# Cell and shared experts of a gated cross-attention stack in one block, chunk 0 ahead of the last pairs

## The chip, the cores and the metric

The program runs on one core of a Trainium2 chip (trn2). The metric is device time in microseconds of one execution; the median of several runs counts. The engines are TensorE (PE), VectorE (DVE), ScalarE (ACT), GpSimd (POOL) and SyncE (SP), which issues most DMAs. Each runs its own list of instructions in order and waits on semaphores for the others.

## The reference

Input `x` is 16 sequences of 128 tokens of 256 numbers, with a context of the same shape. Everything is float32. Four parts follow each other, each added to `x` through the tanh of a gate:

```python
x = x + tanh(g_xattn[0]) * L0_xattn(layernorm(x), ctx, ctx)   # mLSTM cell, 8 heads, layernorm of its output times ln_scale
x = x + tanh(g_ffn[0])   * L0_ffn(layernorm(x))               # 2 shared experts and top 2 of 8 routed experts, hidden 512
x = x + tanh(g_xattn[1]) * L1_xattn(layernorm(x), ctx, mask)  # attention, 16 heads
x = x + tanh(g_ffn[1])   * L1_ffn(layernorm(x))               # shared expert and 16 routed ones in groups
```

The change touches the first part and the beginning of the second. The cell's core, for each sequence and head, is

```python
C = (q @ k.T / sqrt(DH)) * exp(log_D - max_log_D)
h = (C / (maximum(abs(C.sum(-1)), exp(-max_log_D)) + EPS)) @ v
h = (h - mean(h)) / sqrt(var(h) + LN_EPS) * ln_scale
```

and an expert is `silu(x @ w1.T) * (x @ w3.T) @ w2.T`.

## The kernel before, in words

**The front** (`front`) loads `x`, constants and context, normalises `x`, and works out the cell's gates.

**The cell** (`cell`) is a block of its own, with a barrier of all engines ahead of it and behind it. The 16 sequences go in 8 pairs. For pair i: `exponents` adds the broadcast row of maxima and a mask (VectorE for pairs 1 and 2, GpSimd for 3 to 7, one instruction of 2048 columns); ScalarE makes 16 exponentials into `dmat`; TensorE makes the scores; VectorE multiplies the two (`weights`, L497); TensorE makes the values and sums; ScalarE copies them (`keep_out`); TensorE turns them back to token rows (`turn_back`) into PSUM; VectorE finishes (`finish`): it forms the denominator, scales in PSUM, takes statistics (L521, L524) and writes `h = (back - mean) * ln_tanh` (L528). `finish` of pair i stands behind `weights` of pair i+2; the last two stand at the end. GpSimd also splits the first shared block of weights, `raw`, into a high and a low half (`piece`, 8 pieces of 384 columns, L365 and L367), one behind `exponents(5)`, one behind `exponents(6)`, six at the end. A float32 operand is kept as two float32r halves, and three products replace one.

**The shared experts** (`shared_feed_forward`) open the next block. The tokens go in 4 chunks of 4 tiles. For each chunk: `h` is scaled by the reciprocal deviation and added to `X` (`add_h` on VectorE for chunks 0 and 1; `unscale` on ScalarE and `add` on GpSimd for 2 and 3), then `statistics`, Sqrt (`deviation`), `normalise`, `turn` into two PSUM banks, and `keep_hi` and `keep_lo` into halves. The feed-forward runs in 32 units, 8 to a chunk: `gate_up(u)` (12 multiplies of 512 columns), silu, `hidden(u)`, the cast `hhi`, `low(u)`, and `down(u)` (12 multiplies of 256 columns). TensorE's order is `gate_up(u+1)` and then `down(u)`. The work on later chunks, the router, and the splits of the routed experts' weights are written by hand behind certain units of each engine's list.

**The router** stands behind `gate_up(9)` (`u == 8`): logits for all tokens, then on VectorE `logits_by_token`, `second`, `choose`, `tiles_of`, `positions` (`u == 12`) and `slot_weights` (`u == 13`). GpSimd waits for the slots and their weights and then scatters 2 x 16 tiles of rows by indirect DMA (L1694). SyncE waits for all of them, stores chunk 2 of `X` to `sums`, and loads experts 0 and 1 into the place of the scattered rows. ScalarE's split of the last parts of experts 6 and 7 (unit 27) waits for that store.

**The routed experts** (`routed_tiles`, 39 tiles) and the attention stage follow. `cell` and the shared experts have eight PSUM banks between them; VectorE and ScalarE read PSUM, GpSimd does not.

Of the kernel before, what the change touches and what calls it, by code (L numbers as in the profile page):

```python
# [16 lines left out]
KT = D // 128  # L17
# [38 lines left out]
def front(nc, X, XNT, ctxT_all, val, cst, small, loads, wg, bg, xn, AT, ET, m_dram, v_loaded, expo0, mrow1, m_first):  # L56
# [5 lines left out]
    with ExitStack() as ctx:  # L62
# [34 lines left out]
        def _(sp):  # L97
# [13 lines left out]
            sp.dma_start(val[:], ctx_dram.rearrange("s p d -> p s d")).then_inc(v_loaded, 16)  # L111
            sp.wait_ge(max_ready, 1)
# [175 lines left out]
def cell(nc, X, XNT, ctxT_all, val, v_loaded, m_dram, cst, AT, ET, g_in, g_tanh, lns, ln_tanh, tiles, h, hmv, hstd,  # L288
         raw, w0_dram, w1_dram, sw0, rw_raw, rw, blank_rows, xg_dram, sum_dram, slots_blank, sums_blank, m_first,
# [10 lines left out]
    PIECES = 8  # L300

    SPLIT = {5: 1, 6: 1, 7: 6}
    with ExitStack() as ctx:
        sb = lambda n, s, d=F32: ctx.enter_context(nc.sbuf_tensor("c_" + n, s, d))
        sem = lambda n: ctx.enter_context(nc.semaphore("c_" + n))
# [5 lines left out]
        hstats = sb("hstats", [128, B, 6])  # L311
        score = ctx.enter_context(nc.psum_tensor("c_score", [128, 4 * 512], F32))
        pvT = two(lambda n: ctx.enter_context(nc.psum_tensor("c_" + n, [128, 512], F32)), "pvT")
        back = ctx.enter_context(nc.psum_tensor("c_back", [128, 2 * 512], F32))
        m_loaded, raw_loaded = two(sem, "m_loaded"), sem("raw_loaded")
        ones_ready, oT_ready, back_ready = sem("ones_ready"), sem("oT_ready"), sem("back_ready")
        score_ready, expo_dve, expo_pool = sem("score_ready"), sem("expo_dve"), sem("expo_pool")
        dmat_ready, cmat_ready, pv_ready, h_ready = sem("dmat_ready"), sem("cmat_ready"), sem("pv_ready"), sem("h_ready")
        tanh_ready, var_ready, split_done = sem("tanh_ready"), sem("var_ready"), sem("split_done")
        block = ctx.enter_context(nc.Block())  # L320
# [17 lines left out]

        @block.sync
        def _(sp):  # L340
            for i in range(2, PAIRS):
                wait_expo(sp, i - 2)
                for q in range(2):
                    sp.dma_start(mrow[i % 2][:, q].rearrange("p k r t -> p (k r t)"),
                                 m_dram.rearrange("(b h) t -> b (h t)", b=B)[2 * i + q:2 * i + q + 1]
                                 .broadcast_to([128, NH0 * 128])).then_inc(m_loaded[i % 2], 16)
                if i == 3:
                    sp.dma_start(raw, w0_dram).then_inc(raw_loaded, 16)
# [7 lines left out]
        def _(pool):  # L356
# [27 lines left out]
            split(rw_raw, flat(rw[:, 0]), flat(rw[:, 1]))  # L384
            for i in range(BY_DVE, PAIRS):
                exponents(i)
                if i == min(SPLIT):
                    pool.wait_ge(raw_loaded, 16)
                done = sum(SPLIT.get(past, 0) for past in range(i))
                for n in range(done, done + SPLIT.get(i, 0)):  # L390
                    piece(n)

        @block.tensor
        def _(pe):
# [33 lines left out]
            def turn_back(i):  # L428
                if i < PAIRS - 2:
                    wait(pe, h_ready, i)  # L430
# [19 lines left out]
            for _ in range(6):  # L450
                pe.matmul(pvT[0][:], cst[:, C_ID:C_ID + 128], cst[:, 0:512], start=True, stop=True)

        @block.scalar
        def _(act):
# [8 lines left out]
            for i in range(PAIRS):  # L463
# [9 lines left out]
                if i >= 2:  # L473
                    keep_out(i - 2)
            for i in (PAIRS - 2, PAIRS - 1):
                keep_out(i)
            for first, end in ((0, PAIRS - 1), (PAIRS - 1, PAIRS)):
                act.wait_ge(var_ready, end)
                act.activation(hstd[:, 2 * first:2 * end], hmv[:, 2 * first:2 * end, 1], ACT.Sqrt,
                               bias=cst[:, C_EPS:C_EPS + 1])  # L480

        @block.vector
        def _(dve):
# [18 lines left out]
            def finish(i):  # L502
                dve.wait_ge(back_ready, i + 1)
                back = back_of(i)
                sums = back[:, 512:768].rearrange("p (n x) -> p n x", x=DH0)[:, :, 0:2]
                pairs = lambda a: a.rearrange("p q (r x) -> p (q r) x", x=2)
                dve.scalar_tensor_tensor(pairs(den[:]), sums, CELL_EPS * ROOT0,
                                         ET[:, 16 * i:16 * i + 16].rearrange("p (n x) -> p n x", x=2),
                                         ALU.subtract, ALU.max, reverse0=True)
                dve.drain()  # L510
                dve.scalar_tensor_tensor(pairs(den2[:]), sums, CELL_EPS * ROOT0, pairs(den[:]), ALU.add, ALU.max)
                dve.drain()
                dve.reciprocal(rden[:], den2[:])
                dve.drain()
                out = [back[:, q * D:(q + 1) * D] for q in range(2)]
                for q in range(2):
                    dve.tensor_tensor(out[q].rearrange("p (h d) -> p h d", h=NH0), out[q].rearrange("p (h d) -> p h d", h=NH0),
                                      rden[:, q].rearrange("p (h o) -> p h o", o=1).broadcast_to([128, NH0, DH0]), ALU.mult)
                dve.drain()
                for q in range(2):  # L520
                    dve.bn_stats(hstats[:, 2 * i + q, :], out[q])  # L521
                dve.drain()
                for q in range(2):
                    dve.bn_aggr(hmv[:, 2 * i + q, :], hstats[:, 2 * i + q, :])  # L524
                dve.drain().then_inc(var_ready, 1)
                for q in range(2):
                    s = 2 * i + q
# [2015 lines left out]
```

## Time and profile before

| | |
|---|---|
| median of 3 runs | 842.46 us (840.55 to 843.86) |
| the profiled execution | 842.14 us, its span 840.3 us |
| TensorE busy | 780.4 us, 93% |
| VectorE busy | 485.9 us, 58% |
| ScalarE busy | 398.7 us, 47% |
| GpSimd busy | 228.2 us, 27% |
| granted TensorE clock, mean | 0.982 |

The span is the time between the first and last instruction of the profiled execution. Times in the rows are counted from its start. Busy shares are averages over all stages; where the time goes is read from the timeline and the chain around the change.

### The profile page before, as it was taken

The numbers are of one execution on the slowest core, as the hardware profiler recorded it, in microseconds if no ns is written. First come the engines' busy times: TensorE is split into PE (matmuls) and PEld (weight loads), VectorE is DVE, ScalarE is ACT, GpSimd is POOL, SyncE is SP. The second block draws the span as 40 slices with busy tenths as digits, with TensorE's granted clock in tenths as the row PEclk, the third lists the DMA queues.
The fourth block names the chain that finished last, engine by engine and source line by source line (L and its number), as shares of the span: only waits on it lengthen the run. The fifth ranks groups of instructions, "written<-read, shape, count | busy, mean of one in ns | idle before, by whom it ended". The sixth has DMA issues, their size and how long they took to land.

```text
span 840.3 us, 15738 instructions
## 1 busy us (share of the span) xinstructions
PE 780.4 (93%) x5412; PEld 628.7 (75%) x5412; DVE 485.9 (58%) x1607; ACT 398.7 (47%) x817; POOL 228.2 (27%) x208
## 2 busy tenths in 40 slices
PE   8668899999999999999999889998889999999997
PEld 7456487788887888888887545655668878888886
DVE  5488865465474333343333676767676666756544
ACT  5598455144462222222223488888835344243222
POOL 0069210037601222232224248765300000000000
PEclk9989999999999999999999999999999999999999
DMA  8478640024252333433332700202004022050140
GB/s 303 143 267 305 259 192 1 1 94 146 86 186 70 66 66 64 85 74 66 63 51 27 233 1 15 89 2 76 2 4 100 1 67 61 1 127 2 33 94 26
DMA packets 37516, 74.51 MB, mean 89 GB/s; under 512 B 4448, under 2 KB 25568, under 8 KB 35680
## 3 DMA queue, kind: packets, MB, share of 16 engines
q1 hardware_dynamic: 30288, 64.16, 24.5%
q0 software_dynamic: 7152, 9.34, 6.3%
q8 instruction: 46, 0.75, 0.4%
q14 instruction: 30, 0.25, 0.1%
HBM read 59.76 MB, written 19.01 MB: 94 GB/s over the span
## 4 chain that ended last, share of the span: by engine, by line
PE 42%; DVE 14%; issue 13%; ACT 7%; POOL 5%; DMA 4%; DVEq 3%; POOLq 1%; SPq 0%; ACTq 0%
PE t_y_ps L2292 8%; POOL slot_tokens L1694 4%; PE a_turned L999 3%; PE a_score L977 2%; PE t_up L2273 2%; PE t_up L2274 2%; PE t_up L2272 2%; PE a_score L979 2%; PE a_score L978 2%; ACT a_hhi L1175 2%; PE t_gate L2262 2%; PE t_gate L2263 2%; PE t_gate L2264 2%; PE a_turned L903 2%; PE a_proj L876 2%
## 5 line engine op out<-in xcount | busy, mean ns | idle before, releaser
L2232 POOL DMA_INDIRECT sums<-t_y,t_dest x39 | 60.9, 1561 | 167.3 <-DMA sums<-t_y,t_dest 95.7
L2327 ACT CAST t_xT_hi<-t_x_turned 128x256 fp32r<-128x256 f32 x39 | 14.5, 372 | 139.0 <-PE t_x_turned L2253 139.0
L2292 PE MATMUL t_y_ps<-W,t_hidT 128*128 x312 | 73.8, 379 | 0.8 <-ACT t_hidT L2337 0.8
L1175 ACT CAST a_hhi<-a_hid 128x512 fp32r<-128x512 f32 x48 | 29.7, 620 | 86.8 <-DVEq L1461 85.2
L2292 PEld LDWEIGHTS t_y_ps<-W,t_hidT 128*128 128x128 f32 x312 | 59.0, 189 | 10.5 <-issue 1.0
L1307 DVE CUSTOM_DVE_ANT_0 a_sc<-a_score,a_pen 128x128 f32<-128x128 f32 x256 | 56.4, 285 | 7.9 <-PE a_score L891 6.7
L1463 DVE TENSOR_TENSOR a_hlo<-a_hid,a_hhi 128x512 fp32r<-128x512 f32 x48 | 33.3, 693 | 35.1 <-ACT a_hhi L1175 35.1
L1164 ACT ACTIVATE a_act_g<-a_score 128x512 f32<-128x512 f32 x48 | 28.7, 597 | 46.7 <-PE a_score L979 46.5
L2356 DVE TENSOR_TENSOR t_hid<-t_act_g,t_up 128x512 f32<-128x512 f32 x39 | 28.0, 718 | 36.6 <-ACT t_act_g L2332 32.8
L832 POOL TENSOR_TENSOR a_sc<-a_nmx,a_sc 128x512 f32<-128x512 f32 x32 | 33.4, 1043 | 45.2 <-DVE a_nmx L1307 45.1
L2348 DVE TENSOR_TENSOR t_xT_lo<-t_x_turned,t_xT_hi 128x256 fp32r<-128x256 f32 x39 | 16.6, 425 | 43.1 <-ACT t_xT_hi L2327 43.1
L2367 DVE TENSOR_SCALAR t_y<-t_y_ps,t_dest 128x256 f32<-128x256 f32 x39 | 18.9, 484 | 38.6 <-PE t_y_ps L2292 38.6
L1123 ACT ACTIVATE a_pr<-a_sc,a_nmx 128x128 f32<-128x128 f32 x128 | 40.7, 391 | 0.0
L1694 POOL DMA_INDIRECT slot_tokens<-W,slots x32 | 35.6, 1112 | 15.0 <-issue 15.0
L903 PE MATMUL a_turned<-cst,a_pr 128*128 128x128 f32 x256 | 38.5, 283 | 0.7 <-ACT a_prT L1130 0.5
L470 ACT ACTIVATE W<-W,AT 128x128 f32<-128x128 f32 x128 | 38.1, 389 | 1.9 <-POOL W L378 1.9
L2262 PE MATMUL t_gate<-whi_main,t_xT_hi 128*128 x78 | 37.3, 478 | 0.3
L1455 DVE TENSOR_TENSOR a_hid<-a_score,a_cb 128x512 f32<-128x512 f32 x32 | 22.1, 691 | 22.0 <-PE a_score L979 18.7
L903 PEld LDWEIGHTS a_turned<-cst,a_pr 128*128 128x128 f32 x256 | 27.7, 142 | 9.5 <-issue 6.7
L2263 PE MATMUL t_gate<-W,t_xT_hi 128*128 x78 | 30.9, 396 | 0.0
L2273 PE MATMUL t_up<-W,t_xT_hi 128*128 x78 | 30.8, 395 | 0.0
L2264 PE MATMUL t_gate<-whi_main,t_xT_lo 128*128 x78 | 30.8, 395 | 0.0
(428 smaller groups left out, 2261.6 us busy)
## 6 DMA issues: line engine op xcount, KB each, us to landing
W<-in_w_dram SPq DMA_DIRECT2D x9, 1536.0 KB, 8.0
a_cb<-comb_rows SPq DMA_DIRECT2D x16, 512.0 KB, 8.5
W<-m_rows SPq DMA_DIRECT2D x14, 512.0 KB, 4.9
slot_tokens<-in_blank_rows_dram SPq DMA_DIRECT2D x1, 5031.0 KB, 19.8
t_x<-slot_tokens SPq DMA_DIRECT2D x39, 129.0 KB, 2.6
a_raw<-in_w_dram SPq DMA_DIRECT2D x3, 1536.0 KB, 7.5
X<-in_x_dram SPq DMA_DIRECT2D x4, 512.0 KB, 6.1
ctxT_all<-in_ctxT_dram SPq DMA_DIRECT2D x4, 512.0 KB, 8.9
```

What stands on the lines that cost most here:

```text
L470: last = act.activation(dmat[i % 2][:, q, k, r], expo[i % 2][:, q, k, r], ACT.Exp, bias=AT[:, at:at + 1], scale=-1.0)
L903: last = pe.transpose(turned[n % 2][:, i * 128:(i + 1) * 128], pr[s % 2][:, g, i], cst[:, C_ID:C_ID + 128])
L1123: last = act.activation(pr[s % 2][:, g, i], sc[s % 2][:, g, i], ACT.Exp, bias=nmx[s % 2][:, g, i:i + 1], scale=-1.0)
L1175: act.copy(hhi[u % 2][:], hid[u % 2]).then_inc(hhi_ready, 1)
L1307: last = dve.tensor_tensor_reduce(sc[s % 2][:, r, i], score[:, r * 512 + i * 128:r * 512 + (i + 1) * 128], pen[c % 2][:, j], -1.0, 3e38, A ...
L1694: pool.indirect_dma_start(xg_dram, bass.IndirectOffsetOnAxis(ap=slots[:, k, s:s + 1], axis=0), XN[:, s, :], None).then_inc(done, 16)
L2232: pool.indirect_dma_start(sum_dram, bass.IndirectOffsetOnAxis(ap=dest[p][:, 0:1].bitcast(U32), axis=0), y[p][:], None, compute_op=ALU.add) ...
L2262: pe.matmul(gate[p][:], xT_hi[p][:, k], W_hi[0][:, ds(e, 1), cols], start=(k == 0), stop=False)
L2263: pe.matmul(gate[p][:], xT_hi[p][:, k], W[:, ds(e, 1), cols].bitcast(F32R), start=False, stop=False)
L2264: last = pe.matmul(gate[p][:], xT_lo[p][:, k], W_hi[0][:, ds(e, 1), cols], start=False, stop=(k == KT - 1))
L2273: pe.matmul(up[p][:], xT_hi[p][:, k], W[:, ds(e, 1), cols].bitcast(F32R), start=False, stop=False)
L2292: last = pe.matmul(y_ps[p][:, 0:D], hidT[p][:, h], W[:, ds(e, 1), at:at + D], start=(h == 0), stop=(h == HT - 1))
```

## The change

It joins the cell and the shared experts in one block, and reorders what stands at the junction. By part:

- `finish` becomes `take` (denominator and scaling, now written to `h` in SBUF) and `measure` (statistics, and for pairs 0 to 4 the subtraction and the multiply by `ln_tanh`, from `h` to `h`). For pairs 5 to 7 GpSimd does that in `scaled`, two instructions of 512 columns a pair.
- VectorE finishes pairs 0 to 4 in the cell's loop, then makes chunk 0 ready, and takes pairs 5 to 7 between its steps; the statistics of 6 and 7 come in unit 0.
- `h` is added by GpSimd for chunks 1, 2 and 3; chunk 1 to 3 are normalised and turned in later units.
- `raw` is loaded in the front; three of the split's pieces come ahead of `exponents(3)`, five behind `exponents(7)`.
- PSUM banks are laid out so that `gate_up(0)` can write where pair 5 was, and chunk 1 uses the banks of chunk 0.
- The router and its steps come two units later, `slot_weights` one.
- Filler multiplies of TensorE: 6 and 7 before, 2 after.

```diff
@@ cell
-    PIECES = 8
-    SPLIT = {5: 1, 6: 1, 7: 6}
+    PIECES, EARLY = 8, 3
+    BY_POOL = 5
+        def deviation(act, first, end):
+            act.wait_ge(var_ready, end)
+            act.activation(hstd[:, 2 * first:2 * end], hmv[:, 2 * first:2 * end, 1], ACT.Sqrt,
+                           bias=cst[:, C_EPS:C_EPS + 1]).then_inc(hstd_ready, 1)
+        def scaled(pool, i):
+            pool.wait_ge(var_ready, i + 1)
+            both, shape = h[:, 2 * i:2 * i + 2, :], [128, 2, D]
+            pool.tensor_tensor(both, both, hmv[:, 2 * i:2 * i + 2, 0:1].broadcast_to(shape), ALU.subtract)
+            pool.drain()
+            pool.tensor_tensor(both, both, ln_tanh.rearrange("p (o d) -> p o d", o=1).broadcast_to(shape), ALU.mult
+                               ).then_inc(scaled_ready, 1)
+        def take(dve, i):
+            dve.wait_ge(back_ready, i + 1)
...
+            for q in range(2):
+                last = dve.tensor_tensor(h[:, 2 * i + q, :].rearrange("p (h d) -> p h d", h=NH0),
+                                         back[:, q * D:(q + 1) * D].rearrange("p (h d) -> p h d", h=NH0),
+                                         rden[:, q].rearrange("p (h o) -> p h o", o=1).broadcast_to([128, NH0, DH0]), ALU.mult)
+            last.then_inc(back_free, 1)
+            dve.drain()
+        def measure(dve, i):
+            for s in (2 * i, 2 * i + 1):
+                dve.bn_stats(hstats[:, s, :], h[:, s, :])
+            dve.drain()
+            for s in (2 * i, 2 * i + 1):
+                dve.bn_aggr(hmv[:, s, :], hstats[:, s, :])
+            dve.drain().then_inc(var_ready, 1)
+            if i < BY_POOL:
+                for s in (2 * i, 2 * i + 1):
+                    dve.scalar_tensor_tensor(h[:, s, :], h[:, s, :], hmv[:, s, 0:1], ln_tanh, ALU.subtract, ALU.mult)
@@ cell, gpsimd
+            pool.wait_ge(raw_loaded, 16)
+            for n in range(EARLY):
+                piece(n)
             for i in range(BY_DVE, PAIRS):
                 exponents(i)
-                if i == min(SPLIT):
-                    pool.wait_ge(raw_loaded, 16)
-                done = sum(SPLIT.get(past, 0) for past in range(i))
-                for n in range(done, done + SPLIT.get(i, 0)):
-                    piece(n)
+            for n in range(EARLY, PIECES):
+                piece(n)
+            scaled(pool, BY_POOL)
@@ cell, tensor
-            for _ in range(6):
-                pe.matmul(pvT[0][:], cst[:, C_ID:C_ID + 128], cst[:, 0:512], start=True, stop=True)
@@ cell, vector
-                if i >= 2:
-                    finish(i - 2)
-            for i in (PAIRS - 2, PAIRS - 1):
-                finish(i)
+                if 2 <= i < PAIRS - 1:
+                    take(dve, i - 2)
+                    measure(dve, i - 2)
@@ shared experts, sync
+            sp.wait_ge(cmat_ready, PAIRS)
             for e in range(under_tokens, 5):
+                if e == 4:
+                    sp.wait_ge(pv_ready, 2 * PAIRS)
                 sp.dma_start(W[:, e, :], w_dram[NSH0 + e]).then_inc(w_loaded[e], 16)
@@ shared experts, gpsimd
-            for c in LATE:
-                add(c)
+            add(1)
+            scaled(pool, PAIRS - 2)
+            scaled(pool, PAIRS - 1)
+            add(2)
+            add(3)
@@ shared experts, tensor (gate_up(0) takes the high halves first, then waits for lo_ready)
-            busy(5)
+            busy(2)
             turn(0, 0)
             turn(0, 1)
-            busy(2)
             gate_up(0)
             for u in range(NU - 1):
                 gate_up(u + 1)
-                if u == 8:
+                if u == 10:
                     router()
-                elif u == 11:
+                elif u == 13:
                     counts()
                 down(u)
-                if u == 8:
+                if u == 10:
                     turn_logits()
-                if u in (2, 4, 6):
-                    turn(u // 2, 0)
-                    turn(u // 2, 1)
+                if u in (4, 7, 8):
+                    c = (4, 7, 8).index(u) + 1
+                    turn(c, 0)
+                    turn(c, 1)
@@ shared experts, scalar
                 if u == 0:
-                    unscale(LATE[1])
-                elif u == 3:
+                    block1_hi(0)
+                    block1_hi(1)
+                elif u == 1:
+                    unscale(2)
+                elif u == 2:
+                    cell_deviation(act, PAIRS - 2, PAIRS)
+                    deviation(1, 2)
+                elif u == 4:
+                    unscale(3)
+                elif u == 6:
                     deviation(2, 4)
-                elif u == 12:
+                elif u == 13:
                     act.wait_ge(diff_ready, 1)
@@ shared experts, vector
+            cell_rstd(1, 0, PAIRS - 3)
             add_h(0)
             statistics(0)
             normalise(0)
-            add_h(1)
+            take(dve, PAIRS - 3)
+            measure(dve, PAIRS - 3)
             keep_lo(0, 0)
             keep_lo(0, 1)
-            statistics(1)
+            take(dve, PAIRS - 2)
+            take(dve, PAIRS - 1)
...
                 if u == 0:
-                    statistics(2)
+                    cell_rstd(2, PAIRS - 3, PAIRS - 2)
+                    measure(dve, PAIRS - 2)
+                    measure(dve, PAIRS - 1)
+                elif u == 1:
                     block1_lo(0)
-                elif u == 1:
-                    normalise(1)
                     block1_lo(1)
                 elif u == 2:
                     block1_lo(2)
-                    statistics(3)
+                    statistics(1)
                 elif u == 3:
+                    normalise(1)
+                    cell_rstd(3, PAIRS - 2, PAIRS)
+                elif u == 4:
+                    statistics(2)
...
-                elif u == 11:
+                elif u == 13:
                     tiles_of()
-                elif u == 12:
+                elif u == 14:
                     positions()
-                elif u == 13:
                     slot_weights()
```

## Rows read from the trace of the kernel before

**Rows 1.** Chain that ended last, shared experts: start us, us, what.
```profile
178.53 0.22 POOLq L1702
...
232.15 3.45 DMA sums<-X
...
256.15 3.13 DMA t_x<-slot_tokens
```

**Rows 2.** Waits, 84 to 262 us: waiting <- releaser: us, times, longest.
```profile
POOL W L1690 <- DVE slot_weight L2039: 64.4, 1, 64.4
...
PE f_y L1786 <- ACT f_hhi L1845: 2.8, 3, 1.5
```

**Rows 3.** Timeline of VectorE, units 12 and 13: start us, us, instruction, idle before.
```profile
174.76 0.18 DVE L2018 CAST slots<-f_slot_f 128x32 uint32<-128x32 f32 x1
...
177.42 0.17 DVE L2033 TENSOR_SCALAR f_m<-f_e 128x16 f32<-128x16 f32 x1
...
178.30 0.17 DVE L2039 TENSOR_TENSOR slot_weight<-slot_weight,f_e 128x16 f32<-128x16 f32 x1
```

**Rows 4.** Timeline of ScalarE, the silus of two units.
```profile
227.29 0.60 ACT L1840 ACTIVATE X<-f_gate 128x512 f32<-128x512 f32 x1 [0.78 <-PE f_up L1769]
...
231.47 0.60 ACT L1840 ACTIVATE f_hid<-f_gate 128x512 f32<-128x512 f32 x1 [0.50 <-PE f_up L1769]
```

**Rows 5.** Timeline of VectorE, cell and junction.
```profile
61.75 0.88 DVE L528 SCALAR_TENSOR_TENSOR W<-c_back,hmv,ln_tanh 128x256 f32<-128x256 f32 x2
...
80.82 2.35 DVE L497 TENSOR_TENSOR W<-c_score,W 128x1024 f32<-128x1024 f32 x2
...
86.75 0.17 DVE L507 SCALAR_TENSOR_TENSOR c_den<-c_score,ET 128x16 f32<-128x16 f32 x1
...
88.40 0.76 DVE L521 BATCH_NORM_STATS2 c_hstats<-c_score 128x6 f32<-128x256 f32 x2
...
89.62 0.88 DVE L528 SCALAR_TENSOR_TENSOR W<-c_score,hmv,ln_tanh 128x256 f32<-128x256 f32 x2
...
94.47 0.25 DVE L2066 RECIPROCAL f_hrstd<-hstd 128x16 f32<-128x16 f32 x1 [0.32 <-PEq L303]
```

**Rows 6.** Timeline of all engines, first turn to first `down`.
```profile
100.65 0.63 PE L1725 MATMUL f_choice<-cst,W 128*128 128x128 f32 x4 [1.64 <-ACT W L1830]
...
102.54 0.68 DVE L1935 TENSOR_TENSOR x_halves<-f_y,x_halves 128x512 fp32r<-128x512 f32 x1
...
109.81 0.64 PE L1786 MATMUL f_y<-sw0hi,f_hlo 128*128 128x256 f32 x4
```

**Rows 7.** Timeline of ScalarE, a switch of tables.
```profile
126.22 1.28 ACT L1840 ACT_TABLE_LOAD   x1
127.51 0.60 ACT L1840 ACTIVATE W<-f_gate 128x512 f32<-128x512 f32 x1
```

**Rows 8.** Single source lines: ns min/median/max, first and last start us, forms.
```profile
L1685 POOL TENSOR_TENSOR X<-X,W x8: 715/726/1712, 96.6 to 113.5; 128x256 f32<-128x256 f32 x8
...
L1947 DVE TENSOR_TENSOR sw1lo<-W,sw1hi x3: 1219/1221/1591, 111.3 to 119.1; 128x1024 fp32r<-128x1024 f32 x3
...
L1294 DVE TENSOR_SCALAR a_xn<-X,a_mean_var,a_rstd x4: 404/616/1131, 490.4 to 522.5; 128x256 f32<-128x256 f32 x4
...
L832 POOL TENSOR_TENSOR a_sc<-a_nmx,a_sc x32: 1035/1040/1142, 485.5 to 606.3; 128x512 f32<-128x512 f32 x32
```

**Rows 9.** Timelines of GpSimd and ScalarE in the cell.
```profile
53.16 9.05 POOL L378 TENSOR_TENSOR W<-W,cst 128x2048 f32<-128x2048 f32 x2 [2.56 <-DMA W<-m_rows]
...
57.73 4.79 ACT L470 ACTIVATE W<-W,AT 128x128 f32<-128x128 f32 x16 [0.95 <-POOL W L378]
...
85.68 1.01 POOL L367 TENSOR_TENSOR sw0lo<-W,sw0hi 128x384 fp32r<-128x384 f32 x1
```

**Rows 10.** Stretches: us, busy us (count) of PE, PEld, DVE, ACT, POOL, PEclk, DMA.
```profile
60.60:63.00 2.40, 0.01 (x2) 0.01 (x1) 2.20 (x7) 2.40 (x9) 2.40 (x2) 1.00 0.61 244
63.00:66.10 3.10, 3.08 (x38) 2.65 (x42) 2.87 (x7) 3.10 (x12) 2.96 (x2) 0.52 0.85 292
```

More of the change, by code:

```diff
@@ L53, with front @@
 C_END = _cols
-def front(nc, X, XNT, ctxT_all, val, cst, small, loads, wg, bg, xn, AT, ET, m_dram, v_loaded, expo0, mrow1, m_first):
+def front(nc, X, XNT, ctxT_all, val, cst, small, loads, wg, bg, xn, AT, ET, m_dram, v_loaded, expo0, mrow1, m_first,
+          raw, w0_dram, raw_loaded):
     half = CH // 2
@@ L285, in front, with cell @@
     return range(min(numbers), max(numbers) + 1)
-def cell(nc, X, XNT, ctxT_all, val, v_loaded, m_dram, cst, AT, ET, g_in, g_tanh, lns, ln_tanh, tiles, h, hmv, hstd,
-         raw, w0_dram, w1_dram, sw0, rw_raw, rw, blank_rows, xg_dram, sum_dram, slots_blank, sums_blank, m_first,
+def cell(nc, block, sems, X, XNT, ctxT_all, val, v_loaded, m_dram, cst, AT, ET, g_in, g_tanh, lns, ln_tanh, tiles, h, hmv, hstd,
+         raw, raw_loaded, w1_dram, sw0, rw_raw, rw, blank_rows, xg_dram, sum_dram, slots_blank, sums_blank, m_first,
          raw1_loaded, dead):
@@ L429, in turn_back @@
                 if i < PAIRS - 2:
-                    wait(pe, h_ready, i)
+                    wait(pe, back_free, i)
                 else:
@@ L474, in _ @@
                     keep_out(i - 2)
+            deviation(act, 0, BY_POOL)
             for i in (PAIRS - 2, PAIRS - 1):
                 keep_out(i)
[L477 to L480, printed above, removed]
         @block.vector
@@ L500, in weights @@
                 last.then_inc(cmat_ready, 1)
[L502 to L527, printed above, removed]
-                    last = dve.scalar_tensor_tensor(h[:, s, :], out[q], hmv[:, s, 0:1], ln_tanh[:], ALU.subtract, ALU.mult)
-                last.then_inc(h_ready, 1)
             dve.wait_ge(tanh_ready, 1)
-            dve.tensor_scalar(ln_tanh[:], lns[:], g_tanh[:, 0:1], None, ALU.mult)
+            dve.tensor_scalar(ln_tanh, lns, g_tanh[:, 0:1], None, ALU.mult)
             for i in range(PAIRS):
@@ L1580, in shared_feed_forward @@
     HALF = CH // 2
-    LATE = (2, 3)
+    LATE = (1, 2, 3)
+    PAIRS = B // 2
+    (cell_deviation, scaled, take, measure), (hstd_ready, scaled_ready), (cmat_ready, pv_ready, back_free, split_done) = past
     with ExitStack() as ctx:
@@ L1625, in shared_feed_forward @@
         expert_f, expert_c = (raw1[0:1, 1536 + 64 * n:1536 + 64 * n + NT] for n in range(2))
-        gate, up = two(pb, "gate"), two(pb, "up")
+        gate, up = zip(*[(pb(f"gate{q}"), pb(f"up{q}")) for q in range(2)])
         y_bank = [pb(f"y{n}") for n in range(3)]
```

142 lines of the change are left out of this document (90 added, 52 removed).

## The prediction

> **What bounds the stretch now.** I read the chain of work that ended last first, over the shared experts. There the reader is to see that TensorE, busy as it is, does not end the stage: the chain enters GpSimd at 178.5 us (32 scatters of token rows into slots), then through the store of chunk 2 that SyncE issues behind them (232.15, 3.45 us), then through the weight splits that wait for that store, and comes out in the first tiles of the routed experts at 256.15 [rows 1]. The table of waits names what the scatters themselves waited for: GpSimd sat 64.4 us for `slot_weight` from VectorE [rows 2]. So the end of `slot_weights` on VectorE (178.47) sets the end of the stage, 78 us later, by a chain that the change does not shorten. VectorE's timeline of units 12 and 13 shows what stands ahead of it: `positions` ends at 174.9, and the four operations of `slot_weights`, a unit later, run from 177.42 to 178.47, 1.05 us together [rows 3]. A unit lasts 4.18 us where TensorE sets the pace (two silus in a row, 227.29 and 231.47) [rows 4].
>
> The second place is the junction of cell and shared experts. VectorE ends the last `weights` of the cell at about 83.1, finishes pairs 5, 6 and 7, and only at 94.47 begins on chunk 0 [rows 5]; the first turn of chunk 0 is at 100.65 and the first `down` ends at 110.4 [rows 6].
>
> **The router moves.** It comes two units later (8 to 10, counts 11 to 13, positions 12 to 14): +8.4 us. `slot_weights` now follows `positions` in one unit instead of a unit later: of the 3.5 us between the two ends (174.9 to 178.47) only 1.05 stay, so -2.5. The scatters then start 5.9 us later, less what the units gain; call that gain G. The end of the stage moves by 5.9 - G. If the units gained more than that, TensorE would come early and stand at unit 27, where the splits wait for the store, and the end would still follow the scatters.
>
> **Junction, gain 11.4.** Chunk 0 needs the steps from 94.47 to the turn at 100.65, 6.2 us [rows 5, 6]; they now follow the last `weights` at 83.1, so the turn is at 89.3. The copies out of PSUM end near 91.2, and `gate_up(0)` may begin on the high halves. VectorE is the longer way: from 88.7 it does `take(5)` (1.65, the spacing of 86.75 and 88.40), its statistics (1.2, 88.40 to 89.62) [rows 5], two low halves (0.7 each, the second at 102.54 [rows 6]), `take(6)` and `take(7)` (3.3), to 96.2. `hidden(0)` and the cast add 1.4, `down(0)` 1.4: 99.0 against 110.4, 11.4 less. The barrier between the blocks is inside this.
>
> **Units 0 to 9, loss 3.7.** What was finished in the junction now lies in the units. Going through ScalarE and VectorE in their written order with the same durations, TensorE stands 0.8 us at `down(1)` (ScalarE splits block 1 in unit 0), 0.8 at `down(2)` (VectorE has two thirds of the low half ahead of `hidden(2)`), 2.9 at `down(3)` (Sqrt for pairs 6 and 7 and chunk 1 waits for `statistics(1)`, then the table for silu), 0.8 at the turns of chunk 2, 0.4 at `down(8)`, which now waits for both halves of chunk 0 to leave the banks, and 0.8 at the turns of chunk 3: 6.5. Before, it stood 2.8 at its `down`s [rows 2]; 3.7 is the difference. The units have one more pair of table switches than before.
>
> A table load takes 1.28 us and the next operation starts at its end, 127.51 [rows 7]. The Trainium skill, ScalarE: Activation LUTs, What ACT_TABLE_LOAD costs, adds a drain of about 1.38 us to each of them; the sum would be some 2.8 us later by it for the added pair, and the rows here show no such gap.
>
> **Cell, loss about 6.5.** This is the term that decides. `finish` multiplied out of PSUM: one tensor in PSUM, `ln_tanh` in SBUF. `take` now writes `h` to SBUF, and for pairs 0 to 4 `measure` multiplies `h` by `ln_tanh`, both in SBUF. What VectorE and GpSimd do to each other then is in the trace at two places [rows 8]. GpSimd's adds take 0.73 us each, but one of the eight took 1.71, and it lies beside the first of VectorE's splits of block 1 (111.3), which has two SBUF inputs and took 1.59 instead of 1.22. One normalisation of VectorE took 1.13 instead of 0.40 in the attention stage, where GpSimd's masked scores take 1.04 each. Each time one engine waited until the other's instruction was done. The Trainium skill says it so, too (SBUF — State Buffer, Who interferes with whom): a VectorE instruction with two SBUF inputs and a GpSimd one that reads SBUF exclude each other for a whole instruction. By that rule the trace agrees (1.71 against 0.73).
>
> GpSimd's `exponents` are single instructions of 4.5 us (two in 9.05) [rows 9]. Which of them does a multiply meet? Before, pair 1's multiply began at 61.75, and ScalarE's 16 exponentials of pair 4 ran from 57.73 to 62.5 [rows 5, 9]. The end of these lets `exponents(6)` start; before it came later, at 64.1, behind a piece of the split; now that piece is gone. In the new order the exponentials end near 63.0. From one multiply to the next lie a `weights` of 2.3 and the 2.9 from 86.75 to 89.62 [rows 5]. Pair 0's multiply (ready near 56.2) meets `exponents(4)`, which ends near 57.2: +1.4 with the 0.35 that the early pieces (1.0 us at most each [rows 9]) put on `exponents(2)`. Pair 1's is then ready at 63.15, and `exponents(6)` starts at 63.1 and holds to 67.6. If VectorE wins that race, pair 2's multiply at 69.1 meets `exponents(7)` (68.7 to 73.2) in its stead. So one full block of 4 to 4.5 comes in either case. Later multiplies lie beside the pieces of the split, 0.8 and 1.0 us long: 0.5 to 1.5 for each, for two or three pairs. By the one way the last `weights` ends at 89.0, by the other at 91.6, against 83.1: a loss of 5.9 to 8.5. I take 6.5, near the lower end, because the first pieces may pass between two multiplies without a wait. From below the bound is 0: no multiply ever waits.
>
> The early pieces themselves fit GpSimd's idle time ahead of `exponents(3)`; the last five end near 85, ahead of the new start of `gate_up(0)` in a cell that is 6.5 longer, and the next load into `raw` behind them lands before its use. The load of `raw` moves into the front, where it is the last of a long row of loads, and its first use is in the cell: nothing for it; it would cost if the store of the row maxima, which is queued behind it on SyncE, found it still running. SyncE then holds the loads of experts 2 to 4 until the last `weights`; none is used before unit 16: nothing either. Fewer filler multiplies: TensorE's granted clock after 2.4 us of standing was 0.52 for 3.1 us [rows 10], which is the 1.2 GHz level; `gate_up(0)` at half pace ends inside the 2.2 us that `hidden(0)` is late anyway, a second one would cost up to 2.3. I take 0.
>
> **Units, port, loss 1.** In units 1 and 2 `low`, and the split of block 1, lie beside GpSimd's scaling of pairs 5 to 7 and three chunks of adds (0.73 us each, the scalings about 1.1 by GpSimd's 4.5 us for 2048 columns). Each meeting costs up to 1.1; I take 1.0, bounds 0 and 2.5. Putting the scaling of pairs 5 to 7 on GpSimd takes 0.9 each off VectorE and is counted above.
>
> **The sum.** G = 11.4 - 3.7 - 6.5 - 1.0 = 0.2. The end moves by 5.9 - 0.2 = +5.7 us. The profiled execution took 842.1 (its span 840.3), which is 0.4 below the median of the runs, so 847.8 on its scale and 848.2 on the median's. Behind the stage only the order of PSUM banks changes, and the routed tiles' first turn still goes to a bank that chunk 3 leaves free: 0.
>
> **Rivals.**
> - *The multiplies hardly wait* (the place is the cell, the price the 6.5 and the 1.0; it decides when no block of 4 us occurs). For it: the rows of contention are with GpSimd instructions of 0.7 to 1.1 us, none with one of 4.5. Against it: they fit whole-instruction waits. Then G = 7.7, the end moves by -1.8: 840.7, not slower.
> - *The end does not hang on the scatters.* Then it moves by -G: 842.3 with the port's losses, 834.8 without. For it: between the silus of units 26 and 27 TensorE keeps its 4.18 [rows 4]. Against it: the chain, and splits that stand behind the store in ScalarE's order [rows 1].
> - *The junction comes cold or the port costs its upper end*: cell 8.5, units 2.5, half clock 2.3 more. Then G = 11.4 - 2.3 - 3.7 - 8.5 - 2.5 = -5.6 and the end moves by 11.5: 854.
>
> **How the numbers follow.** Forecast 0.56, multiplies hardly wait 0.22, end not on the scatters 0.08 (half of it with each G), cold or upper end 0.14. The forecast's own range, from the cell's bounds of 5.9 to 8.5, the units' 0 to 2.5 and 2 us for a sum over fifteen units, is 844.5 to 851.5. The range reaches to the first rival's 840.7 with a little under it, and up to 852. Half a per cent is 4.2 us, about what a measurement of this kernel can tell from no change: the edges are 838.3 and 846.7. Above lie two thirds of the forecast and all of the last rival, 0.53; below, some of the second and a tail of the first, 0.1; the rest, 0.37, is between.
>
> **What would show it.** In the profile after: VectorE's multiply by `ln_tanh` takes 0.48 us in some pairs and 4 us in one or two; the last `weights` of the cell ends near 89.5; `down(0)` ends near 105.5; `slot_weights` ends near 184 and the last scatter near 237; ScalarE stands at the split of the sixth and seventh experts' last parts. Wrong it would be if every multiply takes 0.5 to 1 us (then the first rival), or if the chain that ended last leaves GpSimd out.

## The result, and the profile after

The changed kernel took 848.4 us (median of 4 runs, 845.9 to 852.8), the kernel before 841.5 in the same runs: a ratio of 1.0079, with a 95% interval of 1.005 to 1.0108. It is 0.8% slower, an interval that leaves out no change, and the forecast of 848.2 stands. Most stops of the sum can be read in the profile after (846.1 us, span 843.8). One execution of the kernel before, in the series of experiments 1 to 4, took 1277.2 us at a mean granted clock of 0.555 and is in no ratio here.

The timeline of VectorE in the cell, `ln_tanh` multiplies (two of 0.48 us each where nothing stops them) and the last `weights`; to be set beside [rows 5]:

```profile
55.81 1.51 DVE L386 SCALAR_TENSOR_TENSOR W<-W,hmv 128x256 f32<-128x256 f32 x2
...
62.37 0.88 DVE L386 SCALAR_TENSOR_TENSOR W<-W,hmv 128x256 f32<-128x256 f32 x2
...
68.31 5.43 DVE L386 SCALAR_TENSOR_TENSOR W<-W,hmv 128x256 f32<-128x256 f32 x2
...
78.78 1.88 DVE L386 SCALAR_TENSOR_TENSOR W<-W,hmv 128x256 f32<-128x256 f32 x2
...
86.87 2.35 DVE L540 TENSOR_TENSOR W<-c_score,W 128x1024 f32<-128x1024 f32 x2
```

GpSimd's timeline of the same stretch, its `exponents`:

```profile
57.24 4.56 POOL L425 TENSOR_TENSOR W<-W,cst 128x2048 f32<-128x2048 f32 x1 [0.60 <-DMA W<-m_rows]
63.41 9.08 POOL L425 TENSOR_TENSOR W<-W,cst 128x2048 f32<-128x2048 f32 x2 [1.60 <-DMA W<-m_rows]
```

Pair 1 began at 62.37, before `exponents(6)` at 63.41, and lost nothing. Pair 2 was ready at 68.31, 0.4 us after `exponents(7)` had begun (half way in the two of 9.08), and its two multiplies lasted 5.43 instead of 0.88. Pair 0 lost 0.6 and pair 3 1.0. The last `weights` ends at 89.22, before at 83.17 [rows 5]: 6.05 us.

TensorE's timeline from the first turn to unit 3, the longest waits and the end of the first `down`; beside [rows 6]:

```profile
95.17 0.63 PE L1748 MATMUL f_choice<-cst,W 128*128 128x128 f32 x4 [0.27 <-ACT W L1873]
97.01 0.47 PE L1796 MATMUL f_gate<-x_halves,sw0hi 128*128 128x512 f32 x1 [0.77 <-ACT x_halves L1879]
...
104.51 0.64 PE L1827 MATMUL f_y<-sw0hi,f_hlo 128*128 128x256 f32 x4
...
114.25 0.39 PE L1827 MATMUL f_y<-sw0hi,f_hhi 128*128 128x256 f32 x1 [1.17 <-ACT f_hhi L1888]
117.23 0.47 PE L1806 MATMUL f_gate<-x_halves,sw1hi 128*128 128x512 f32 x1 [1.03 <-DVE sw1lo L1995]
122.61 0.58 PE L1827 MATMUL f_y<-sw0hi,f_hhi 128*128 128x256 f32 x1 [2.40 <-ACT f_hhi L1888]
```

`down(0)` ends at 105.15, before at 110.45: from the last `weights` it is 15.93 us now and was 27.28. In the units TensorE then waits, in short waits of 0.2 and 0.3 and in these three: 1.2, 1.0 and 2.4 us.

The stretches behind the longest of these waits (us, busy us and count of TensorE, its weight loads, VectorE, ScalarE and GpSimd, granted clock, share of DMA, GB/s):

```profile
120.00:123.00 3.00, 0.60 (x3) 0.39 (x3) 1.10 (x2) 1.74 (x3) 0.00 (x0) 0.91 0.00 0
123.00:126.00 3.00, 3.00 (x14) 2.90 (x14) 2.09 (x7) 1.57 (x3) 0.00 (x0) 0.52 0.00 0
126.00:129.00 3.00, 3.00 (x17) 2.52 (x17) 2.25 (x9) 2.68 (x6) 0.67 (x1) 1.00 0.00 0
```

A granted clock of 0.52 is the 1.2 GHz level; in the 3 us before TensorE was busy for 0.60 us. The prediction has no such term for the units.

The end of the stage, from the waits of GpSimd, from the timelines, and from the chain that ended last; beside [rows 1, 2]:

```profile
POOL W L1710 <- DVE slot_weight L2087: 53.8, 1, 53.8
```

```profile
184.73 0.18 DVE L2087 TENSOR_TENSOR slot_weight<-slot_weight,f_e 128x16 f32<-128x16 f32 x1
...
233.17 0.60 ACT L1883 ACTIVATE f_hid<-f_gate 128x512 f32<-128x512 f32 x1 [0.50 <-PE f_up L1808]
...
235.60 0.96 POOL L1714 DMA_INDIRECT slot_tokens<-W,slots  x1 [0.31 <-issue]
238.39 0.36 SPq L1676 DMA_DIRECT2D sums<-X  x1
241.93 1.14 ACT L1912 CAST whi_last<-W 128x512 fp32r<-128x512 f32 x2 [6.17 <-DMA sums<-X]
```

```profile
238.39 3.46 DMA sums<-X
...
263.04 3.02 DMA t_x<-slot_tokens
```

`slot_weights` ends at 184.91 (178.47 before, +6.4), the store of chunk 2 starts at 238.39 (+6.2) and the load of the first routed tile at 263.04 (256.15 before, +6.9). ScalarE stood 6.17 us for that store, behind the silu of unit 27 (233.17). The medians differ by the same 6.9; that they do so to a tenth is chance, since the four executions lie between 845.9 and 852.8. In this one execution the span grew by 3.5 only, since everything behind 263 took 580.8 us where it had taken 584.2; in a second profile of the same kernel it took 583.4, and the span was 847.1.

### The profile page after: what moved, and what is told of

It reads as the page before. It is cut to its first block, busy times and chain, and to the rows that moved or that the text cites. A ratio compares the mean times of both kernels' runs of the same rounds, so it can differ in the third digit from the quotient of the medians.

```text
span 843.8 us, 15700 instructions
## 1 busy us (share of the span) xinstructions
PE 774.3 (92%) x5390; PEld 625.0 (74%) x5390; DVE 491.0 (58%) x1599; ACT 402.6 (48%) x824; POOL 243.5 (29%) x218
## 4 chain that ended last, share of the span: by engine, by line
PE 44%; DVE 17%; issue 12%; ACT 8%; POOL 6%; DVEq 4%; DMA 2%; POOLq 1%; ACTq 0%; SPq 0%
PE t_y_ps L2356 8%; POOL slot_tokens L1714 4%; PE a_turned L1013 3%; ACT a_hhi L1189 2%; PE a_score L991 2%; PE a_turned L917 2%; PE t_up L2336 2%; PE t_up L2338 2%; PE t_up L2337 2%; PE a_score L993 2%; PE a_score L992 2%; PE t_gate L2326 2%; PE t_gate L2327 2%; PE t_gate L2328 2%; PE a_proj L890 2%
```

## The experiments

Each ratio is to the kernel before, run on the same chip; experiments 1 to 4 ran on one chip, 5 to 8 on a second, 9 and 10 on a third.

**1. The multiply back in PSUM.** For pairs 0 to 4 `take` leaves its result in PSUM and the statistics and the multiply by `ln_tanh` read it there, so the PSUM bank is given back behind the multiply and no longer behind `take`; the rest is the changed kernel.

```diff
-                last = dve.tensor_tensor(h[:, 2 * i + q, :].rearrange(...)
+                out = h[:, 2 * i + q, :] if i >= BY_POOL else back[:, q * D:(q + 1) * D]
+                last = dve.tensor_tensor(out.rearrange(...)
...
-                    dve.scalar_tensor_tensor(h[:, s, :], h[:, s, :], hmv[:, s, 0:1], ln_tanh, ALU.subtract, ALU.mult)
+                    last = dve.scalar_tensor_tensor(h[:, s, :], source(s), hmv[:, s, 0:1], ln_tanh, ALU.subtract, ALU.mult)
```

> The changed kernel, but pairs 0 to 4 scale and take their statistics in PSUM again, so that the multiply by ln_tanh has one input in SBUF. Theory (the multiply and GpSimd's 4.5 us instructions shut each other out): no multiply in the cell takes more than 0.5 us, the cell's last weights ends at 83 instead of 89.1, slot_weights at 179 instead of 184.9, and the time is 6 us under the changed kernel, 842.4, ratio to before 1.001. Rival (the cell is longer for another reason, the clock or the moved load): last weights stays at 89, time 848.4. Rival (the end of the stage does not hang on the scatters): the cell shortens by 6 and the end by less than 3.

841.6 us, ratio 0.9991 (0.9974 to 1.0009). VectorE's timeline has all five as they were:

```profile
61.97 0.88 DVE L389 SCALAR_TENSOR_TENSOR W<-c_back,hmv,W 128x256 f32<-128x256 f32 x2
67.89 0.88 DVE L389 SCALAR_TENSOR_TENSOR W<-c_back,hmv,W 128x256 f32<-128x256 f32 x2
```

The last `weights` ends at 83.24 and `slot_weights` at 179.16, 5.8 before the changed kernel's. So the loss in the cell comes from where `h` lies, and it reaches the end; that a GpSimd instruction is what the multiply waits for is shown by experiment 6.

**2. The router one unit earlier** in the changed kernel (unit 9; counts, exponentials and the steps behind them 1 earlier each).

```diff
-                if u == 10:
+                if u == 9:
                     router()
-                elif u == 13:
+                elif u == 12:
                     counts()
...
```

> The changed kernel with the router and all its steps one unit earlier (9 instead of 10, positions and slot_weights at 13). Nothing else moves. Theory (the end of the shared experts hangs on the end of slot_weights): slot_weights ends 4.2 us earlier, near 180.7, the scatters and the store with it, and the time is 844.2, ratio 1.003. Rival (the end hangs on the units of TensorE, whose work is the same): 848.4, ratio 1.008.

844.3 us, ratio 1.0036 (1.0018 to 1.0054); `slot_weights` ends at 181.83, in a cell that was 1.0 longer: 4.1 for one unit. The cell was longer because here the race went the other way. VectorE's timeline has the full block at pair 1, as the other branch of the prediction has it, and none at pair 2:

```profile
62.40 5.18 DVE L386 SCALAR_TENSOR_TENSOR W<-W,hmv 128x256 f32<-128x256 f32 x2
...
72.64 2.09 DVE L386 SCALAR_TENSOR_TENSOR W<-W,hmv 128x256 f32<-128x256 f32 x2
```

**3. Both edits together.**

> Both edits on the changed kernel: multiply out of PSUM, router at 9. Theory: the two add, since they are terms of one sum: slot_weights ends near 174.7, time 838.2, ratio 0.996, faster than both kernels. Rival (with the scatters 10 us earlier TensorE or ScalarE sets the end): half of the router's 4.2 is lost, 840.3, and ScalarE's wait for the store at unit 27 is gone.

837.6 us, ratio 0.9956 (0.9939 to 0.9974): faster than both kernels. `slot_weights` ends at 173.98 and the load of the first tile starts at 251.73, 4.4 earlier than in the kernel before. The two edits add up. ScalarE still stands 2.87 us for the store, so the scatters still end the stage: the silu of unit 27 is 25.94 us ahead of that load, where experiment 10 has 24.35 with nothing waiting, so some 1.6 us are left to gain by a still earlier router.

**4. The kernel before with only the router moved,** to units 10, 13 and 14, `slot_weights` joined to `positions`.

```diff
-                if u == 8:
+                if u == 10:
                     router()
...
-                elif u == 12:
+                elif u == 14:
                     positions()
-                elif u == 13:
                     slot_weights()
```

> The kernel before with the router's part of the change alone: router at 10, counts at 13, positions and slot_weights at 14. Theory: slot_weights ends 5.9 us later (184.4), the scatters with it, ScalarE stands 6 us longer for the store at unit 27, time 847.4, ratio 1.007. Rival (TensorE's work is the same and sets the end): 841.5, ratio 1.000.

848.0 us, ratio 1.007 (1.0048 to 1.0092). `slot_weights` ends at 186.11, in a cell that ended 1.8 later than before's in this execution: 5.8 us for the move, against 5.9 in the sum. The edit does not touch the cell, so this 1.8 is a difference between executions of the same instructions. VectorE's timeline:

```profile
82.63 2.36 DVE L497 TENSOR_TENSOR W<-c_score,W 128x1024 f32<-128x1024 f32 x2 [1.95 <-PE c_score L403]
```

The last `weights` waited for the scores, which TensorE made at a low granted clock (0.63 from 81 to 84) behind a wait of 2.71 us, 2.09 us for the 32 multiplies; in the profile of [rows 5] that wait was 1.61 us, the clock 1.00 and the scores took 1.17. The profile of experiment 10, whose cell is that of the kernel before too, shows it again (2.43 us, 0.54, last `weights` at 84.78). So the 83.17 with which this document compares is the earliest of three.

**5. The kernel before with only `h` in SBUF.** The first multiply of `finish` writes `h`; the statistics and the second multiply read it there, for all eight pairs, and the bank is given back behind the first.

```diff
-                out = [back[:, q * D:(q + 1) * D] for q in range(2)]
+                out = [h[:, 2 * i + q, :] for q in range(2)]
...
```

> The kernel before with one thing of the change: finish scales into h in SBUF and multiplies h by ln_tanh there, for all pairs. Theory (whole-instruction exclusion): GpSimd's exponents of pairs 4 and 5 stand back to back here (53.2 to 62.2), so pair 0's two multiplies meet one each, and the later pairs meet an exponents or pieces: cell's last weights 6 to 13 us later than 83.1, time about 850, ratio 1.010. Rival (the two engines share the port and slow each other by a share): each multiply takes up to twice its 0.48 us, 5 us at most over the cell but no single one over 1 us, time 844. Rival (no contention): 841.5.

850.0 us, ratio 1.011 (1.0082 to 1.0138). VectorE's timeline:

```profile
55.84 7.26 DVE L530 SCALAR_TENSOR_TENSOR W<-W,hmv,ln_tanh 128x256 f32<-128x256 f32 x2
...
68.15 2.52 DVE L530 SCALAR_TENSOR_TENSOR W<-W,hmv,ln_tanh 128x256 f32<-128x256 f32 x2
```

Here pair 0 lost 6.4 us: its two multiplies were ready inside the two `exponents` that GpSimd runs one behind the other, 53.61 to 62.81. The last `weights` ends at 92.79 (+9.6) and `slot_weights` at 188.08 (+9.6). One operand's place costs the kernel before as much as the whole change does, or more; the two intervals overlap.

**6. `exponents` in four instructions of 512 columns** in the changed kernel.

```diff
+                for n in range(4):
+                    part = slice(4 * n, 4 * n + 4)
+                    last = pool.tensor_tensor(expo[...][:, part], mrow[...][:, part], cst[...].broadcast_to([128, 4, 128]), ALU.add)
+                last.then_inc(expo_pool, 1)
...
```

> The changed kernel with GpSimd's exponents of 2048 columns cut into four instructions of 512. Same work, same order. Theory (a multiply waits for the end of the instruction that it meets): no multiply takes over 1.7 us, the cell loses about 3 instead of 6.1, last weights at 86, time 845.4, ratio 1.004. Rival (the wait is for bandwidth, so only the amount of work counts): one pair still loses over 4 us and the time stays 848.4, ratio 1.008.

846.1 us, ratio 1.0048 (1.0031 to 1.0066). GpSimd's and VectorE's timelines:

```profile
64.18 10.30 POOL L427 TENSOR_TENSOR W<-W,cst 128x512 f32<-128x512 f32 x8 [1.34 <-DMA W<-m_rows]
```

```profile
63.04 0.88 DVE L386 SCALAR_TENSOR_TENSOR W<-W,hmv 128x256 f32<-128x256 f32 x2
...
68.97 1.91 DVE L386 SCALAR_TENSOR_TENSOR W<-W,hmv 128x256 f32<-128x256 f32 x2
```

GpSimd runs without a gap from 64.18 to 74.48, and pair 2 gets in between two of its instructions. No pair loses more than 1.3 us now, about one instruction of 1.29; all together lose 3.9 where the changed kernel's lost 6.2, and the last `weights` ends at 86.98, 2.2 earlier. The wait is for one instruction, not for the row of them. The rival, that cutting them brings nothing, falls.

**7. GpSimd's arithmetic taken out of the units** of the changed kernel. The scaling of pairs 5 to 7 and the adds to X work on 4 columns of 256 only, so this part of the computation is left out.

```diff
-                    last = pool.tensor_tensor(X[:, s, :], X[:, s, :], h[:, s, :], ALU.add)
+                    last = pool.tensor_tensor(X[:, s, 0:4], X[:, s, 0:4], h[:, s, 0:4], ALU.add)
...
```

> The changed kernel with GpSimd's scaling of pairs 5 to 7 and its adds of h to X for chunks 1 to 3 cut to four columns of each row: most of that arithmetic is left out, every wait stays. Theory (VectorE's two-input instructions in units 1 to 5 wait for GpSimd): low(1), low(2) and the three splits of block 1 go back to 0.69 and 1.22 us, slot_weights ends 2.5 us earlier (182.4), time 845.9, ratio 1.005. Rival (the units are bound by ScalarE's tables and casts there, and the waits are hidden): slot_weights at 184.9, 848.4.

844.8 us, ratio 1.0037 (1.002 to 1.0054). VectorE's timelines, first of the changed kernel, then of this one:

```profile
108.14 1.39 DVE L2098 SCALAR_TENSOR_TENSOR f_hlo<-f_hid,f_hhi 128x512 fp32r<-128x512 f32 x1 [0.73 <-ACT f_hhi L1888]
109.45 3.45 DVE L1995 TENSOR_TENSOR sw1lo<-W,sw1hi 128x1024 fp32r<-128x1024 f32 x2
114.23 1.19 DVE L2098 SCALAR_TENSOR_TENSOR f_hlo<-W,f_hhi 128x512 fp32r<-128x512 f32 x1 [0.73 <-ACT f_hhi L1888]
115.34 1.75 DVE L1995 TENSOR_TENSOR sw1lo<-W,sw1hi 128x1024 fp32r<-128x1024 f32 x1
```

```profile
108.32 0.69 DVE L2098 SCALAR_TENSOR_TENSOR f_hlo<-f_hid,f_hhi 128x512 fp32r<-128x512 f32 x1 [0.73 <-ACT f_hhi L1888]
108.93 2.35 DVE L1995 TENSOR_TENSOR sw1lo<-W,sw1hi 128x1024 fp32r<-128x1024 f32 x2
112.61 0.69 DVE L2098 SCALAR_TENSOR_TENSOR f_hlo<-W,f_hhi 128x512 fp32r<-128x512 f32 x1 [0.73 <-ACT f_hhi L1888]
113.22 1.22 DVE L1995 TENSOR_TENSOR sw1lo<-W,sw1hi 128x1024 fp32r<-128x1024 f32 x1
```

Five instructions, with only `hidden(2)` between them, lost 0.7, 1.1 (two together), 0.5 and 0.5 us to GpSimd. TensorE's wait for `down(2)` (1.17) is gone and `gate_up(4)` starts at 114.58 instead of 117.23, in a cell that was 0.2 longer: the meetings with GpSimd cost the units 2.8 us, as much as the five lost. `slot_weights` ends at 180.76. The clock stayed at 1.00 here, to which the remaining 1.5 us is put down (experiment 9 has the same size for it).

**8. `statistics(1)` ahead of the last low half of block 1,** in the kernel of experiment 3, to shorten the wait for Sqrt and table.

```diff
                 elif u == 2:
-                    block1_lo(2)
                     statistics(1)
+                    block1_lo(2)
```

> Multiply out of PSUM and router at 9, and in unit 2 VectorE does statistics(1) ahead of the last third of block 1's low half. Theory: the Sqrt and the silu behind it start 1.8 us earlier, gate_up(4) starts 1.8 us later, and down(3) about 0.9 us earlier: slot_weights near 173.1, time 836.7, ratio 0.9945. Rival (gate_up(4) then stands in front of down(3) and gives it all back): 837.6, as without the swap.

838.2 us, ratio 0.9952 (0.9934 to 0.997), no different from experiment 3. The wait before `down(3)` went and the one before `gate_up(4)` grew from 1.01 to 2.47. And the stretches behind it (columns as above) show the low clock:

```profile
111.00:114.00 3.00, 0.77 (x5) 0.53 (x4) 2.80 (x9) 1.53 (x4) 0.57 (x1) 0.91 0.00 0
114.00:117.00 3.00, 2.75 (x7) 2.21 (x8) 1.31 (x3) 1.63 (x3) 0.00 (x0) 0.50 0.00 0
```

**9. Does the low clock belong to the arrangement?** Three kernels profiled a second time, unchanged.

> The changed kernel, profiled a second time, with nothing edited. In the first profile the units 0 to 9 lost 6.0 us where the prediction had 4.7 (3.7 of arrangement and 1.0 of port); 4.5 us of the 6.0 are TensorE waits, and from 123 to 126 us, right behind the longest wait (2.40 us before 122.61), the granted clock of TensorE was 0.52, which is 1.4 us of lost time. Theory C: the fall of the clock belongs to the waits of this arrangement; it comes again within some microseconds of the same place, and slot_weights ends at 184.9 give or take 0.5. Rival D: it varies from execution to execution at the same waits; then a profile without it ends slot_weights at about 183.4, and the remaining 0.3 is all that the prediction's unit term missed.

> The kernel with the multiply back in PSUM and the router at unit 9, profiled a second time. Its first profile had the same waits in units 0 to 9 as the changed kernel (1.2, 1.0 and 2.4 us) and no fall of the granted clock there (1.00 in every 3 us stretch from 99 to 135). Theory C (the clock follows the waits): the first profile would be the exception, and this one shows a stretch near 0.5 or 0.65 between 115 and 126, with slot_weights at about 175.3. Rival D (it varies): 1.00 again or not, slot_weights at 173.8 without it.

> The kernel with the statistics of chunk 1 ahead of the last low halves of w1, profiled a second time. In its first profile the wait of TensorE before down(3) was gone (2.4 us), the one before gate_up(4) had grown from 1.0 to 2.5 us, and the granted clock was 0.50 from 114 to 120: about 3 us lost, slot_weights at 176.4 where the kernel without the swap had 173.8. If that fall comes again, the swap's 0.9 us are paid away by the clock each time; if it does not, slot_weights ends near 173.0 and the swap is worth 0.8 us, too little for these rounds to have told.

Both theories had a part. The stretches of experiment 3's kernel, its first profile and then its second, with the same waits to within 0.03 us:

```profile
114.00:117.00 3.00, 0.91 (x4) 0.40 (x3) 0.69 (x1) 2.19 (x3) 0.00 (x0) 1.00 0.00 0
117.00:120.00 3.00, 2.72 (x18) 2.50 (x19) 1.90 (x7) 1.80 (x4) 0.00 (x0) 1.00 0.00 0
```

```profile
114.00:117.00 3.00, 0.60 (x4) 0.23 (x3) 0.94 (x2) 1.90 (x3) 0.00 (x0) 1.00 0.00 0
117.00:120.00 3.00, 3.00 (x15) 2.81 (x15) 2.16 (x7) 1.57 (x3) 0.00 (x0) 0.56 0.00 0
```

From `gate_up(4)` to the end of `slot_weights` it is 62.07 us in the first and 63.53 in the second: the fall costs 1.5. It came in both profiles of the changed kernel, and in 7 of the 10 profiles that have the new order of units; the three without it are experiments 6 and 7 and the first of experiment 3. So it follows these waits mostly, not always. (Experiments 6 and 7 had other waits ahead of the one of 2.4: 1.7 and 0.5 us, and 0.3 and 0.3.) The two profiles of experiment 3's kernel come from two chips. The first chip had the fall in experiments 1 and 2 and not in 3, the second in 8 and not in 6 and 7, the third in all three repetitions; no single kernel was seen with and without it on one chip, so that the chip has a part in it is not ruled out. Experiment 8's kernel had it both times, for 2.5 us and 1.3, worked out from the same stretch (62.18 and 60.96 us, against the 62.07 of experiment 3 less its later wait of 2.37). That is more than the 0.9 that its swap was to give. In the second profile of the changed kernel pair 1 was the blocked one (5.18 us at 62.41), where in the first it was pair 2. GpSimd's timeline there fits a race that is settled by a fraction of a microsecond:

```profile
62.55 4.75 POOL L425 TENSOR_TENSOR W<-W,cst 128x2048 f32<-128x2048 f32 x1 [0.65 <-ACT W L516]
```

`exponents(6)` was released by ScalarE at 62.55, 0.14 us behind VectorE's start at 62.41, and came in between its two multiplies. In the first profile it waited until 63.41 for the load of its row maxima, and VectorE was through.

**10. `slot_weights` joined to `positions` in the kernel before,** the router where it was.

```diff
                     positions()
-                elif u == 13:
                     slot_weights()
```

> The kernel before, with slot_weights in the same unit as positions (12) and not one later, the router left where it was; nothing else. The prediction took 2.5 us off the price of the router's move for this joining, and has the end of the stage hang on slot_weights. The exponents are there at 173.45 and positions ends at 174.94, so slot_weights ends at about 175.9 where it was 178.47. Theory (the end hangs on slot_weights): 839.2, ratio 0.997, the last wait of ScalarE for the store of chunk 2 at 1.62 grows or the cast itself comes 2.5 earlier. Rival (the end hangs on something else, the units themselves or the store): no change, ratio 1.000, the cast still at 235.7.

841.8 us, ratio 0.9999 (0.9986 to 1.0012): the theory fell. `slot_weights` did end 2.6 us earlier beside its own first turn (177.46, the turn at 102.25, against 178.47 and 100.65), and the store of chunk 2 followed (228.99). ScalarE no longer waited for it. But the load of the first tile stayed where it was beside that turn, and the chain that ended last no longer holds a scatter:

```profile
245.95 1.43 PE f_y L1786 x12
251.62 0.69 DVE W L2063
253.32 2.40 DVE W L2147 x4
255.72 1.57 DVE X L2152 x4
257.79 3.02 DMA t_x<-slot_tokens
```

ScalarE's timeline has the silu of unit 27:

```profile
233.44 0.60 ACT L1840 ACTIVATE f_hid<-f_gate 128x512 f32<-128x512 f32 x1 [0.50 <-PE f_up L1769]
```

With nothing waiting for the store, the silu of unit 27 (233.44 here, 231.47 in [rows 4]) stands 24.35 us ahead of that load. In the kernel before it was 24.68. So in the kernel before the scatters decide by 0.3 us only; right behind them is TensorE's own path. That the load did not come even 0.3 earlier has its reason in the edit: with `slot_weights` in unit 12, ahead of that unit's own work on VectorE, the silu of unit 27 lies 131.19 us behind the first turn instead of 130.82. In the changed kernel it is 29.87: the units by themselves would have ended only 1.4 us later than before (263.04 less 5.5, against 256.15), and 5.5 us are the scatters'.

## Why the prediction came out right

**The move of the router, +5.9:** 5.8 in experiment 4. That the end hangs on `slot_weights` was right for this change, and the 0.3 us of experiment 10 show how narrowly: it holds for a router that comes later, not for one that comes earlier. The rival that the end is not on the scatters is refuted for the changed kernel by its chain, the 6.17 us of ScalarE and experiment 2; as a statement on the kernel before it was nearly true, which the chain alone didn't show, nor did ScalarE's own 1.62 us of waiting there.

**The junction, 11.4:** 27.28 less 15.93 is 11.35. `down(0)` ends at 105.15, forecast 105.5.

**The cell, 6.5:** 6.05, with one full block as the race foretold, and experiment 1 gives 5.8 to 6.0 of it back. The 6.05 is measured from the earliest of three profiles of the kernel before; from the other two (84.99, 84.78), in which TensorE made the last scores at the low clock, it is 4.2 and 4.4. The prediction has no such spread in its start. By the ratios 1.0079 and 0.9991 the multiplies cost 7.4 us, give or take 3 by their intervals. The first rival, that the multiplies hardly wait, falls. The trace agrees with the rule of the Trainium skill (SBUF — State Buffer, Who interferes with whom) that the two exclude each other for a whole instruction: a multiply of 0.48 us took 4.46 here behind one of 4.5, and no pair lost more than 1.3 beside ones of 1.29. One of the prediction's two rows for it doesn't bear on two inputs, though: the normalisation that took 1.13 (L1294, [rows 8]) reads one tensor, `X`, with a mean and a factor for each row of it. It shows that a VectorE instruction with one tensor as input can be long beside GpSimd too; no run here tests that kind.

**Units 0 to 9 and port, 3.7 and 1.0:** together 5.84 instead of 4.7 (from `down(0)` to `slot_weights` 79.76 us, before 68.02, less the 5.9 of the move). This is the term that was mis-sized, and its parts were further off than the sum. The port costs 2.8, above the upper bound of 2.5: each meeting was priced rightly, but in units 1 and 2 five instructions meet GpSimd one behind the other, and what they lose adds up ahead of `gate_up(4)`. The order of the work itself costs 1.5 (experiment 7: 75.43 less 68.02 less 5.9), not 3.7. Of the waits, 0.3 and 0.2 us came at `down(1)` where 0.8 was forecast, 2.4 at `down(3)` for 2.9, 0.54 and 0.56 at the turns of chunks 2 and 3 for 0.8 each, none at `down(8)` for 0.4; and the 2.8 us that are taken off for the kernel before leave out its own 0.55 at a turn (131.81). The remaining 1.5 fits the granted clock, which was left out for the units; the prediction looked for it at the junction only, where it stayed at 1.00.

**The sum:** G was -0.5 where 0.2 was forecast (11.35 - 6.05 - 5.84), and `slot_weights` came 6.4 later, not 5.7. The time between it and the first routed tile was 78.1 us, before 77.7. The mechanism and the sign were right; that the median came within 0.2 us of the forecast is luck. In the units an overpriced order of work (2.2 too much) met an underpriced port (1.8 too little) and a clock fall that was not in the sum (1.5), and the execution with the profile was only 3.9 us above that of the kernel before. The upper edge of the stated range, 851.5, does not follow from its parts as the lower one does: 2.0, 1.5 and 2 above 848.2 would be 853.7.

## What to carry to other kernels

When an intermediate result moves from PSUM to SBUF, look at what reads it next on VectorE: if that instruction now has two inputs in SBUF, each one can wait for the whole of a GpSimd instruction beside it, so price it by the longest of these and not by its own length; keep the operand in PSUM, or cut the long instruction. When a step is moved later on a path, ask also how far behind the next path is, since that alone tells whether moving it earlier would pay: here 2.6 us earlier was worth nothing (0.3 at most, less 0.4 that the edit cost elsewhere) and 5.9 later was paid in full. The gain of this change was there (11.4 us), and of its three costs the cell's could be left out and 4.1 us of the router's saved: with the multiply in PSUM and the router at unit 9 the same reordering is 0.4% faster than the kernel before.

## What was not expected of the hardware

Which multiply is blocked changes from one execution of the same program to the next (pair 2 at 68.31, pair 1 at 62.41); where the load of the row maxima landed late, VectorE was through first; the last `weights` differs by 1.0 us only, since either way one full block comes.

In 7 of 10 profiles the granted clock fell behind a wait of 2.4 to 2.5 us, to between 0.50 and 0.56 over some 3 us, and in the others it did not: the same kernel with the same waits kept 1.00 once and had 0.56 in the 3 us behind them the other time, on another chip. The cell of the kernel before does it too, with waits of 2.71 and 2.43 us, and its last `weights` then ends 1.6 to 1.8 us later. What tips it stays open; no run here varied the waits alone.
